# Turning the aggregated mean by a DMA from an fp16 pair, and the residual sums ahead of the one-hots, in a graph transformer layer

## The reference

```python
xn = layernorm(x)
agg = segment_sum(xn[src], dst, 6250)
ah = agg / deg[:, None]
gnn = xn @ W1.T + b1 + ah @ W2.T + b2
# linear attention: q, k, v = xn @ qkv_weight.T, with relu on q and k
attn = (q @ (k.T v)) / (q . sum(k)) @ proj.T + proj_bias      # per head
x = x + gnn + attn
x = x + ffn(layernorm(x))    # two of eight experts, chosen from one softmax-pooled row
```

## Time and profile before

| | us |
|---|---|
| median of three runs | 1589.22 (1589.18 to 1589.99) |
| the profiled execution | 1589.3 |
| its span in the profile | 1587.5 |
| TensorE busy | 1514.9 (95%) |
| VectorE busy | 1003.3 (63%) |
| POOL busy | 796.0 (50%) |
| ScalarE busy | 604.4 (38%) |

### The profile page before, as it was taken

How to read it: one execution, slowest core, us unless ns; L and a number is a source line. 1 busy time by engine, 2 the same in 40 slices (tenths; PEclk the granted TensorE clock), 3 DMA queues, 4 the chain that set the end, 5 groups by cost and what they waited for, 6 DMA issues and landing times.

```text
span 1587.5 us, 29173 instructions
## 1 busy us (share of the span) xinstructions
PE 1514.9 (95%) x7597; PEld 732.2 (46%) x7598; DVE 1003.3 (63%) x2155; ACT 604.4 (38%) x997; POOL 796.0 (50%) x847
## 2 busy tenths in 40 slices
PE   5999999989999999999999999999999978999997
PEld 2444444444444454444444444454444433444443
DVE  6576622145666676666676666676666656667777
ACT  5777721111323233332233333333333334555554
POOL 4122134746777767777767777767777700000000
PEclk8999999999999999999999999999999989999999
DMA  9977776947777767777767777767777713222223
GB/s 259 245 170 188 180 178 146 218 146 212 235 236 234 235 199 236 233 231 233 233 211 238 234 237 234 235 202 234 236 235 236 235 49 120 93 94 105 101 89 114
DMA packets 166586, 308.64 MB, mean 194 GB/s; under 512 B 71962, under 2 KB 74548, under 8 KB 166236
## 3 DMA queue, kind: packets, MB, share of 16 engines
q0 software_dynamic: 62720, 205.57, 44.5%
q1 hardware_dynamic: 36112, 58.90, 11.7%
q10 hardware_dynamic: 67660, 42.96, 10.7%
HBM read 255.02 MB, written 39.49 MB: 186 GB/s over the span
## 4 chain that ended last, share of the span: by engine, by line
PE 84%; DVE 5%; issue 3%; DVEq 1%; DMA 1%; ACT 0%; SPq 0%; ACTq 0%
PE bank L548 18%; PE bank L553 17%; PE bank L549 17%; PE bank L621 10%; PE bank L622 10%; PE bank L705 2%; PE bank L706 2%; PE bank L707 2%; PE bank L827 1%; PE bank L782 1%; PE bank L789 1%; DVE work L1408 1%; DVE work L1405 1%; DVE ring L1589 1%; DVEq L1223 1%
## 5 line engine op out<-in xcount | busy, mean ns | idle before, releaser
L521 POOL DMA_INDIRECT ring<-table,src_col x784 | 750.1, 957 | 334.4 <-issue 255.7
L621 PE MATMUL bank<-ring,onehot 128*128 x830 | 315.6, 380 | 4.2 <-ACT work L950 2.9
L622 PE MATMUL bank<-ring,onehot 128*128 x830 | 315.5, 380 | 0.0
L1223 DVE TENSOR_TENSOR onehot<-bank,dst_col 128x512 f32 x244 | 168.8, 692 | 122.2 <-issue 89.6
L548 PE MATMUL bank<-wts,xT 128*128 128x512 f16 x588 | 224.1, 381 | 21.9 <-DVE work L1408 13.4
L549 PE MATMUL bank<-wts,xT 128*128 128x512 f16 x588 | 223.7, 380 | 0.0
L950 ACT ACTIVATE work<-bank,rd 128x512 f32<-128x512 f32 x49 | 33.7, 687 | 320.3 <-DVE rd L1256 320.2
L553 PE MATMUL bank<-wts,xT 128*128 128x512 f16 x588 | 151.2, 380 | 0.0
L549 PE MATMUL bank<-wts,work 128*128 128x512 f16 x392 | 148.3, 378 | 0.0
L548 PE MATMUL bank<-wts,work 128*128 128x512 f16 x392 | 148.2, 378 | 0.0
L621 PEld LDWEIGHTS bank<-ring,onehot 128*128 x830 | 81.2, 98 | 100.2 <-issue 10.9
(11 more groups left out here) (278 smaller groups left out, 2578.5 us busy)
## 6 DMA issues: line engine op xcount, KB each, us to landing
ring<-table,src_col POOLq DMA_INDIRECT x784, 3.7
x_rows<-work ACTq DMA_DIRECT2D x49, 256.0 KB, 4.0
work<-in_x ACTq DMA_DIRECT2D x48, 256.0 KB
ring<-x_rows SPq DMA_DIRECT2D x12, 1024.0 KB, 5.2
out_x<-ring SPq DMA_DIRECT2D x12, 1024.0 KB
table<-xT SPq DMA_DIRECT2D x45, 256.0 KB, 3.4
ring<-in_x SPq DMA_DIRECT2D x42, 256.0 KB, 3.5
xT<-in_L_mix_qkv_weight SPq DMA_DIRECT2D x2, 1024.0 KB, 10.1
```

The source lines that it names most:

```text
L521: pool.indirect_dma_start(ring[:, n, :], None, table[:, :], bass.IndirectOffsetOnAxis(ap=ap, axis=0)).then_inc(slot_loaded[n], 16)
L621: mm(ps_agg[:, :], w[:, k, :], rows[:, k, 0:D], start=start, stop=False, skip_group_check=True)
L622: r = mm(ps_agg[:, :], w[:, k, :], rows[:, k, D:2 * D], start=False, stop=stop, skip_group_check=True)
L1223: V.tensor_tensor(onehot[:, bass.ds((q + t) % OG * U, U), :], ps_iota[:, None, :].to_broadcast([P, U, P]), dst_col[:, bass.ds(q % GROUPS * ...
```

## The change

- A slot of `ah` holds an fp16 pair (1024 fp16 in the bytes of 512 fp32). ScalarE writes the high part from the bank; VectorE, in `degrees`, then waits for it and writes the low part from the bank. `ah_made` now follows the low part.
- `turn_ah(t, k)`, at the end of layer t on ScalarE, issues one transposing DMA of 128 by 1024 from the slot into `ahT`, once `ah_made` and the W2 product of the tile before (`w2_used`) are through. TensorE's W2 product waits for its landing. The four transposes L782 and the copies L1045 and L1418 are gone.
- VectorE's layer begins with the two sums of tile i - 2; the one-hots follow.
- TensorE's two register loads of the tile's bounds stand within `query`, no longer ahead of it.
- The last tile's x rows are loaded in layer 48 into a slot of `ah` that is free by then (`x_end`); the mask of the last scores is one operation in place of three.

The diff, cut to its core:

```diff
-        ah = work[:, 7:7 + SLOTS]
+        ah = work[:, 7:7 + SLOTS].rearrange("p k f -> p (k f)").bitcast(F16).rearrange("p (k f) -> p k f", k=SLOTS)
+        x_end = work[:, 7 + (T - SLOTS) % SLOTS]
...
+            def query(t, ahead=None):
+
+                fa = fb = None
                 after(pe, s["w_made"], t)
+                for c in range(C):
+                    mm(ps_q[:, :], tile(t)[:, c, :], wq[:, 0, c, :], start=(c == 0), stop=False)
+                    mm(ps_q[:, :], tile(t)[:, c, :], wq[:, 1, c, :], start=False, stop=False)
+                    if c == 1 and ahead is not None:
+                        fa = block_of(ahead)
+                for c in range(C):
+                    r = mm(ps_q[:, :], tile(t)[:, C + c, :], wq[:, 0, c, :], start=False, stop=(c == C - 1))
+                    if c == 0 and ahead is not None:
+                        fb = block_of(ahead + 1)
...
                 t = i - 1
                 if real(t):
-                    after(pe, s["ah_made"], t + 1)
-                    after(pe, s["ahT_lo"], t)
...
-                    for c in range(C):
-                        r = nc.tensor.transpose(ps_ta[:, c * P:(c + 1) * P], ah[:, (k - 1) % SLOTS, c * P:(c + 1) * P], ident[:])
-                    r.then_inc(s["turned_ah"], 1)
...
-                    after(pe, s["ahT_lo"], t + 1)
+                    after(pe, s["ah_turned"], 16 * t + 16)
...
             def keep_ah(t, k):
 
                 act.wait_ge(s["rd_made"], t + 1)
-                after(act, s["turned_ah"], t - SLOTS + 1)
-                F(ah[:, k % SLOTS, :], ps_agg[:, :], ACT.Copy, scale=rd[:]).then_inc(s["ah_made"], 1)
+                after(act, s["ah_turned"], 16 * t - 16 * SLOTS + 16)
+                F(ah[:, k % SLOTS, 0:D], ps_agg[:, :], ACT.Copy, scale=rd[:]).then_inc(s["ah_hi"], 1)
+
+            def turn_ah(t, k):
+
+                after(act, s["ah_made"], t + 1)
+                after(act, s["w2_used"], t)
+                act.sem_inc(s["act_turn"], 1)
+                act.dma_start_transpose(ahT.rearrange("p a c n -> p (a c) n"), ah[:, k % SLOTS, :]
+                                        ).then_inc(s["ah_turned"], 16)
...
+                    if isinstance(t, int) and t == T - 2:
+                        act.wait_ge(s["ah_turned"], 16 * (T - SLOTS + 1))
+                        F(x_end[TAIL // 32 * 32:P, :], awb[TAIL // 32 * 32:P, :], ACT.Copy, scale=0.0).then_inc(s["x_end_cleared"], 1)
+                        act.wait_ge(s["x_end_cleared"], 1)
+                        for a, b in parts(TAIL):
+                            act.dma_start(x_end[a:b, :], x[(T - 1) * P + a:(T - 1) * P + b, :]).then_inc(s["x_end_loaded"], 16)
...
                 if skew is not None:
                     keep_ah(i + skew, k + skew)
+                t = i
+                if real(t):
+                    turn_ah(t, k)
...
+                after(dve, s["ah_hi"], t + 1)
+                V.scalar_tensor_tensor(out=ah[:, k % SLOTS, D:2 * D], in0=ps_agg[:, :], scalar=rd[:],
+                                       in1=ah[:, k % SLOTS, 0:D], op0=ALU.mult, op1=ALU.subtract).then_inc(s["ah_made"], 1)
...
             def layer(i, skew, k):
+                t = i - 2
+                if real(t):
...
+                    V.scalar_tensor_tensor(out=x2, in0=ps_o[:, :], scalar=mix[:, 1:2], in1=x_end if end else x_in,
+                                           op0=ALU.mult, op1=ALU.add).then_inc(s["sum_steps"], 1)
+                    after(dve, s["sum_steps"], 2 * t + 1)
+                    V.scalar_tensor_tensor(out=x2, in0=ps_b[:, :], scalar=mix[:, 2:3], in1=x2,
+                                           op0=ALU.mult, op1=ALU.add).then_inc(s["x2_made"], 1)
                 if skew is not None:
                     match_rest(i + skew)
```

More of the change, by code:

```diff
@@ L731, in _ @@
                     agg_last(EARLY[i - 2], fb)
-            def query(t):
+            def query(t, ahead=None):
+                fa = fb = None
                 after(pe, s["w_made"], t)
-                three(ps_q[:, :], lambda c: tile(t)[:, c, :], lambda c: tile(t)[:, C + c, :],
-                      lambda c: wq[:, 0, c, :], lambda c: wq[:, 1, c, :], C).then_inc(s["q_made"], 1)
+                for c in range(C):
[7 more added lines that the diff above has]
+                        fb = block_of(ahead + 1)
+                r.then_inc(s["q_made"], 1)
+                return fa, fb
             pe.wait_ge(s["k32_made"], T)
@@ L768, in layer @@
                 if real(t):
-                    if ahead is not None:
-                        fa, fb = blocks_of(ahead)
-                    query(t)
+                    fa, fb = query(t, ahead)
                 if ahead is not None:
@@ L1030, in _ @@
             keep_ah(SKEW, SKEW)
+            turn_ah(0, 0)
             def layer(i, skew, k):
@@ L1043, in layer @@
                 if real(t):
-                    after(act, s["turned_ah"], t + 1)
-                    F(ahT[:, 0], ps_ta[:, :].rearrange("p (c n) -> p c n", c=C), ACT.Copy).then_inc(s["ahT_hi"], 1)
                     after(act, s["turned_p"], t + 1)
@@ L1390, in _ @@
             link(V.memset(acc, 0.0))
+            dve.wait_ge(s["small_loaded"], 48)
+            link(V.scalar_tensor_tensor(out=rowlow[:], in0=rowmask[:], scalar=abb[:], in1=rowlow[:], op0=ALU.mult, op1=ALU.add))
             def layer(i, skew, k):
+                t = i - 2
+                if real(t):
+                    end = isinstance(t, int) and t == T - 1
+                    after(dve, s["lin_made"], t + 1)
+                    after(dve, s["x2_stored"], 16 * t)
+                    if end:
+                        dve.wait_ge(s["x_end_loaded"], 16 * len(parts(TAIL)))
+                    else:
+                        after(dve, s["x_loaded2"], 16 * t + 16)
+                    V.scalar_tensor_tensor(out=x2, in0=ps_o[:, :], scalar=mix[:, 1:2], in1=x_end if end else x_in,
[3 more added lines that the diff above has]
+                                           op0=ALU.mult, op1=ALU.add).then_inc(s["x2_made"], 1)
                 if skew is not None:
@@ L1401, in layer @@
                 if real(t):
-                    after(dve, s["lin_made"], t + 1)
-                    after(dve, s["x2_stored"], 16 * t)
-                    after(dve, s["x_loaded2"], 16 * t + 16)
-                    V.scalar_tensor_tensor(out=x2, in0=ps_o[:, :], scalar=mix[:, 1:2], in1=x_in,
-                                           op0=ALU.mult, op1=ALU.add).then_inc(s["sum_steps"], 1)
-                    after(dve, s["sum_steps"], 2 * t + 1)
-                    V.scalar_tensor_tensor(out=x2, in0=ps_b[:, :], scalar=mix[:, 2:3], in1=x2,
-                                           op0=ALU.mult, op1=ALU.add).then_inc(s["x2_made"], 1)
                     after(dve, s["x2_made"], t + 1)
@@ L1416, in layer @@
                 if real(t):
-                    after(dve, s["ahT_hi"], t + 1)
-                    V.tensor_tensor(ahT[:, 1], ps_ta[:, :].rearrange("p (c n) -> p c n", c=C), ahT[:, 0],
-                                    ALU.subtract).then_inc(s["ahT_lo"], 1)
                     after(dve, s["pT_hi"], t + 1)
```

38 lines of the change are left out of this document (19 added, 19 removed).

## The result

| | before | after |
|---|---|---|
| median of the runs, us | 1589.61 (4 runs, 1589.18 to 1593.27) | 1610.97 (4 runs, 1610.01 to 1613.07) |
| span of the profiled execution | 1587.5 | 1608.2 |

The changed kernel takes 1.0136 times the time of before, 95% interval 1.0123 to 1.0148: 21 us slower. I had forecast 1575.4 us and given slower a chance of 0.13.

The account below looks back on a forecast made before the run. The prediction held that POOL's gathers, 20.2 us a tile against TensorE's 19.3 a layer, limit TensorE's gain in the loop. Terms -7.7 - 2.2 + 0.9 - 4.9 = -13.9 took 1589.3 to 1575.4 us; range 1568 to 1590.

Parts of the forecast that it names:

- POOL's pace: Layer loop: one gather issued every 1.26 us, so a tile's 16 take 20.2 us against TensorE's 19.3 a layer.
- third rival: Layer loop: more DMA traffic slows POOL's gathers, 7 us per 0.01 us each; 1588 at 1.28 us; chance 0.12.
- The transposes: TensorE, each of 48 layers: four transposes of the mean go, 0.47 us a layer, 22.6 us, only partly counting.
- The sum waits: TensorE before the W1 product: 13.4 us of waits in 13 places for the residual sum taken as gone.
- my two terms for the loop: Layer loop: 7.7 us gained through POOL's waits in the three empty layers, 2.2 us after layer 36.
- The price of the one-hots: Each layer: one-hots come later on VectorE, so TensorE waits 0.2 to 1.5 us by tile; 23.3 us paid.
- t0: End of a layer's aggregation; from it the forecast put the second sum at 2.6 us, the first one-hot at 4.5.
- The DMA transpose in full layers: W2 product: 9.5 us from issue to need, landing median 4.5, 4.5 to 6 hidden; costed at nothing.
- first rival: W2 product: the transposing DMA lands late; 1592.6 us at 8.9 us landing, 1603 at 10; chance 0.10.
- The start: Layer 1's first group: the mean's low part is one more VectorE step, delaying POOL's stream as much; +0.9 us.
- The tail: After the last layer: x loaded early gains 4.6 us, merged mask operations 0.3; 4.9 us in all.
- second rival: VectorE: register loads do not overlap the second sum, one-hots 0.75 us later; 1590 us; chance 0.10, half without measurable change.

Follow-up runs that it names:

- e5: Kernel before with sums ahead of one-hots and TensorE's four transposes of the mean left out for all tiles but the first: 1583.26 us, ratio 0.9964.
- e4: Kernel before with one edit, the two sums ahead of the one-hots; transposes stay: 1588.56 us, ratio 0.9986.
- e2: Changed kernel with TensorE's two register loads ahead of the query again: 1608.59 us.
- e10c: Changed kernel without the transposing DMA for all tiles but the first: 1592.17 us, ratio 1.0016.
- e3: Changed kernel with VectorE's two register loads early, ahead of the wait for the turning point: 1587.38 us, ratio 0.9984.
- e7: Kernel before with sums first and the change's two edits of the tail, transposes kept: 1583.17 us, ratio 0.9967.
- e8: Changed kernel with VectorE's register loads early, TensorE's ahead of the query again, and the loop's first tile mended: 1584.54 us, ratio 0.9974.

## Why the prediction was wrong

- **POOL's pace** was right: 946 ns a gather, and ordinary steps of 1.26 us with the transposing DMA as without. My third rival, slower gathers by more traffic, did not happen: the landing rose from 3.7 to 4.1 us, the pace did not.
- **The transposes** are gone as forecast, and that they could count only in part was right too: e5 puts the worth of 22.6 us at 3.5 to 5.3. The sum waits are gone, but their going was worth 2 us (e4). Both together give 5.8 us (1589.03 to 1583.26), less than the 9.9 of my two terms for the loop, even with nothing paid.
- **The price of the one-hots is the step that failed.** I had the second sum at t0 + 2.6 and it came at 2.83; I had 1.9 us from there to the one-hots and it was 2.47. That is 0.8 us later than t0 + 4.5, and the new wait is 39.4 us, not 23.3. Of the 0.57 us in the gap 0.44 are the transposing DMA's, which lengthens a register load; the other 0.13 is that I took one layer's 1.9 for a median of 2.03.
- **What that wait does** was the larger error. With 23.3 us paid, TensorE would have stayed below POOL's 20.2 us a layer. With 39.4 and the small gaps inside the groups, it crosses in the last stretch. From t0 of layer 37 to t0 of layer 48, eleven layers, TensorE took 19.7 us a layer before and 20.5 after. The first row is of before, the others of the changed kernel:

```profile
1063.87 0.64 PE L827 MATMUL bank<-ident,work 128*128 128x128 f32 x4
...
1079.92 0.64 PE L833 MATMUL bank<-ident,work 128*128 128x128 f32 x4
...
1305.49 0.63 PE L833 MATMUL bank<-ident,work 128*128 128x128 f32 x4
```

  (1305.49 - 1079.92 is 225.57, 20.51 each; before, 1280.77 - 1063.87 = 216.90.) In e2 it is 20.5 too, in e10c 20.0 and in e3 19.8: of these four the two above 20.2 are the two that lose about 20 us.

  The ring shows the same. Take the time from the release of a group's place to the group's first gather: in this stretch it grew before, from about 3 us to about 7, and in the changed kernel it shrinks from about 4 us to 2 or 3, and to the bare 0.3 of a gather that has waited in every fourth group. That is why the end of the loop lost 5.7 us more where I had 2.2 gained.

  In the three stretches ahead TensorE only caught up less. The last group of gathers ahead of each long wait starts 6.1, 6.1 and 4.5 us after the release, where it was 7.6, 7.5 and 8.1: 6.5 us in all. The first two layers without a tile took 13.2 and 13.0 us from t0 to t0 and not 11.8, the third 11.4 and not 11.8: 2.2 us. Together that is about the 8.4 us by which POOL's waits grew, where I had 7.7 less.
- **The DMA transpose in full layers** lands in time: no wait at the W2 product there, as forecast. Costing it at nothing failed all the same: in all it costs 18.8 us where VectorE's loads are late (1610.97 against 1592.17). I asked only who waits for it, and looked for its traffic only in the gathers. In the layers without a tile it was late in two of three, and the chain of waits has it:

```profile
582.89 7.17 DMA work<-work
815.74 7.00 DMA work<-work
```

  7 us from issue to landing, not 4.5, which cost TensorE 1.8 and 1.5 us. This is my first rival in small. The Trainium skill, page "VectorE: DVE Perf Modes", section "Rules for kernel authors", advises TensorE for a 128x128 block where PSUM will do; e7 (1583.17 us) against e8 (1584.54) agrees in that the DMA brought nothing. The 1309 ns a block of its section "The three transpose paths" would give an estimated 10.5 us, more than the 7 seen.
- **The start** cost 3.4 us at the loop's first gather, not 0.9: TensorE's first group waited 5.86 us for the low part (L1280), which I had taken as one step more, against 2.87 for ScalarE's copy before. POOL's last gather ahead of the loop was already 2.5 us later (359.2 against 356.7), but kernels with the same first stage differ by up to 2.6 us there, so how much of that is the change is not shown.
- **The tail**: 5.05 us against 4.9, and there in e7 without the DMA, at 3.0 to 5.4 us.
- **My second rival** had the right place and the wrong mechanism. It said that the loads do not overlap the second sum. They do: the gap is 2.03 us whether a reciprocal of 0.16 us or a sum of 0.75 stands ahead. What lengthens it is the DMA's issue. Its price, 1590, was also too low, since it left TensorE under POOL's pace.

## What to carry to other kernels

Before taking work off the busiest engine, find the stream that paces the loop and the margin to it: here 19.3 against 20.2 us a layer, so that relief was worth a quarter of its size or less, while lateness beyond the margin set a new pace. A reordering puts everything in front of what it delays, register loads too; load them ahead of the wait that they would follow. And a DMA that nobody waits for is not free if it is issued just ahead of another engine's register loads, and that engine is late already. Cost such a DMA and the order beside it together, since each alone was milder here than both.

## What the runs showed of the hardware

From the start of the operation ahead, whatever that was, to its next operation VectorE took 2.03 us with two register loads and a branch between them, of which each load is 0.30 to 0.31 us. A load that began about the end of a DMA issue on ScalarE or up to 1.2 us behind it took 0.64 us in the median and up to 1.38 (609 loads in eleven traces), behind a transposing DMA or a plain copy. Of 862 loads at other times all but three took 0.30 to 0.35, 55 of them amid a transposing DMA's packets. With the transposing DMA in the changed kernel the 2.03 us became 2.47. That this time after an issue is what lengthens a load is argued from this timing and from the gap with and without the DMA; what happens in it, and the path that the two share, was not seen.

One transposing DMA of 256 KB took about 1.9 us of all 16 engines' time within 3 us, beside gathers, and took about 7 us to land in the layers without a tile.
